# A two-layer model kernel on one Trainium2 core: expert chunks two deep, and gate factors of the last stage made ahead by GpSimd

## The reference, cut to what matters

```python
scores = sigmoid(x @ gate_weight.T)              # 8 experts of 64
topk_w, topk_idx = top_k(scores, 2)
topk_w = topk_w / topk_w.sum(-1) * 2.5           # combine: 0 off the top 2
hmid = silu(x @ w_gate[e]) * (x @ w_up[e])       # and one shared expert pair
out = sum_e combine[:, e] * (hmid[e] @ w_down[e]) + shared
```

```python
mu, var = mean(y), mean((y - mu) ** 2)
yn = (y - mu) * rsqrt(var + 1e-5) * ln_g + ln_b
y = (yn + D_param * u) * silu(z)
x = x + y @ W_out.T
```

```python
h = gelu(sum_e C1[:, e] * (x @ W1[e].T))         # 12 experts
y = sum_e C2[:, e] * (h @ W2[e].T) + C3 @ b2     # 12 experts
```

## Time and profile before

| | |
|---|---|
| median of 3 runs | 1942.43 us (1942.41 to 1942.91) |
| profiled execution, its own time | 1945.75 us |
| its span, first to last instruction | 1943.7 us |
| mean granted PE clock | 0.928 |
| PE busy | 1597.0 us (82%) |
| DVE busy | 1405.3 us (72%) |
| ACT busy | 1012.8 us (52%) |
| POOL busy | 542.6 us (28%) |

### The profile page before, as it was taken

How to read it: one execution, slowest core, us unless ns; L and a number is a source line. 1 busy time by engine, 2 the same in 40 slices (tenths; PEclk the granted TensorE clock), 3 DMA queues, 4 the chain that set the end, 5 groups by cost and what they waited for, 6 DMA issues and landing times. The chain is left out here.

```text
span 1943.7 us, 37126 instructions
## 1 busy us (share of the span) xinstructions
PE 1597.0 (82%) x11024; PEld 1037.9 (53%) x11024; DVE 1405.3 (72%) x3794; ACT 1012.8 (52%) x2725; POOL 542.6 (28%) x556
## 2 busy tenths in 40 slices
PE   6999999999998997889894881776777746787899
PEld 3666666666664554555562771565556533333444
DVE  4777777777776666666675445999999976778776
ACT  2666666666664332232331227999999921221221
POOL 1111111111111010000000111988888856223100
PEclk9999999999999998999896995889888866889999
DMA  4101110111005500000563001000000000000000
GB/s 131 34 22 32 32 32 22 32 32 32 22 22 173 174 0 1 1 0 0 150 202 109 0 0 61 1 1 1 1 1 0 0 0 1 1 6 6 11 6 17
DMA packets 69345, 66.53 MB, mean 34 GB/s; under 512 B 5695, under 2 KB 66834, under 8 KB 69266
## 3 DMA queue, kind: packets, MB, share of 16 engines
q1 hardware_dynamic: 66598, 64.00, 11.1%
q10 hardware_dynamic: 2668, 1.62, 0.3%
HBM read 61.41 MB, written 4.19 MB: 34 GB/s over the span
## 5 line engine op out<-in xcount | busy, mean ns | idle before, releaser
L1968 PE MATMUL ss_y_ps<-ss_h,ss_diag 128*128 128x256 f32 x1024 | 265.3, 423 | 132.9 <-ACT sc_dt L1886 92.7
L1968 PEld LDWEIGHTS ss_y_ps<-ss_h,ss_diag 128*128 128x128 f32 x1024 | 216.5, 215 | 181.4 <-issue 94.6
L595 ACT ACTIVATE x_probs<-x_probs,x_neg_max 128x257 f32<-128x257 f32 x512 | 253.5, 498 | 64.0 <-DVE x_neg_max L696 64.0
L696 DVE CUSTOM_DVE_ANT_0 x_probs<-x_s_ps,x_mask_b 128x257 f32<-128x257 f32 x512 | 187.3, 423 | 134.9 <-PE x_s_ps L403 134.9
L1870 ACT ACTIVATE ss_decay<-sc_dt,sc_a 128x256 f32 (+1 forms) x496 | 206.7, 470 | 1.8 <-DVE ss_h L1933 1.8
L1924 DVE SCALAR_TENSOR_TENSOR ss_decay<-ss_decay,ss_h 128x1024 f32<-128x1024 f32 x124 | 152.3, 1229 | 28.5 <-ACT ss_decay L1870 28.2
L1880 ACT ACTIVATE ss_come<-ss_dtu,sc_xd 128x256 f32<-128x256 f32 x384 | 162.9, 505 | 6.6 <-POOL ss_dtu L1826 6.6
L413 PE MATMUL x_pT_ps<-all_ident,x_probs 128*128 128x128 f32 x1024 | 163.3, 283 | 0.6 <-DVE x_pT L703 0.6
L1840 POOL TENSOR_TENSOR ss_diag<-all_ident,sc_xd 128x512 f32<-128x512 f32 x128 | 159.8, 1249 | 11.4 <-PE ss_y_ps L1968 1.4
L703 DVE COPY x_pT<-x_pT_ps 128x512 f32<-128x512 f32 x256 | 161.3, 668 | 0.5 <-PE x_pT_ps L413 0.5
L1933 DVE CUSTOM_DVE_ANT_0 ss_h<-ss_come,ss_decay 128x1024 f32<-128x1024 f32 x124 | 150.0, 1210 | 0.0
(11 more groups left out here) (371 smaller groups left out, 3134.8 us busy)
## 6 DMA issues: line engine op xcount, KB each, us to landing
x_ctx_t<-ctxT SPq DMA_DIRECT2D x48, 514.0 KB, 3.8
kept_ctx_t<-ctxT SPq DMA_DIRECT2D x16, 514.0 KB, 7.9
kept_ctx_n<-ctx SPq DMA_DIRECT2D x16, 512.0 KB, 8.2
x_ctx_n<-ctx SPq DMA_DIRECT2D x16, 512.0 KB, 4.2
all_x<-x SPq DMA_DIRECT2D x4, 512.0 KB, 7.5
x_mid<-all_x SPq DMA_DIRECT2D x32, 64.0 KB, 4.0
all_x<-x_mid SPq DMA_DIRECT2D x4, 512.0 KB, 7.8
out<-all_x SPq DMA_DIRECT2D x8, 256.0 KB, 2.0
```

Of the source, the lines that this page charges most:

```text
L595: ins = nc.scalar.activation(probs[p][:, n, :], probs[p][:, n, :], ACT.Exp, scale=-1.0, bias=neg_max[p][:, n:n + 1], accum_out=sums[p][:, ...
L696: vec.tensor_tensor_reduce(probs[p][:, n, :], s_ps[:, c, 0:S2], mask_b[:, :], -1.0, -MASKED, ALU.add, ALU.min, neg_max[p][:, n:n + 1]).the ...
L1968: ins = nc.tensor.matmul(y_ps[p][:, 0:DI], diag[q][:, m, :], h[q][:, m, :], start=(q == 0 and m == 0), stop=(q == NQ - 1 and m == NH - 1))
```

## The change

1. **Experts of layer 0.** The loops are written out. `up` is split: `gate_up` (g with a signal of its own for silu, u) and `weigh` (w, which alone waits for the routing weights). `project` runs two chunks behind instead of one, with three buffers for hid. The first two g and u are issued ahead of the first turn of routing weights. The copies of turned x and of turned routing weights move from DVE to ACT. The moments of the finished group go to chunk 4 of the next.
2. **Scan inputs.** The loads of ln_g, ln_b, D_param, w_o, w_a, w_z and b2 move here, behind x on SP. POOL makes for the first 12 tiles (AHEAD = 3 groups) gz = gate * ln_g and q = (u * D_param + ln_b) * gate: four instructions of 128x256 a tile beside its copy.
3. **Tail.** v becomes (y - mean) * gz (`centred`), then * rstd + q (`finish`), eight DVE instructions of 128x256 a group, at steps 17 to 20 of group n for group n+3. POOL makes gz and q of groups 3 to 7 (`gates`), four instructions of 128x1024 each; those of group n+4 start after step 21 of group n (those of group 3 after the first scale of group 0). The norm of x and the copy of the ranks move from DVE to ACT, turn, address and rank to steps 1, 3, 5 (before 3, 5, 8), and the routing two to three steps earlier; the coefficient chain one step later. The prologue projects groups 0 and 1 before it ranks. The three large loads (two halves of w and spread, 768 KB each) are issued at the start of the tail instead of the scan states; PE waits for them before it turns the first weights.

```diff
             pe.wait_ge(g.experts_in, 16 * N_LOADS)
             turn_x(0)
-            logits(0, 0)
+            logits(0)
+            gate_up(0)
+            gate_up(1)
             turn_weights(0)
...
+            def gate_up(i):
+                n, h, b = i // HC, i % HC, i % 2
+                if h == 0:
+                    pe.wait_ge(xT_sb, n + 1)
+                wait(pe, gate_sb, i - 1)
+                mm(g_ps[b][:, :], w_g[:, h, :], xnT[n % 2][:, :], start=True, stop=True).then_inc(gate_psum, 1)
+                wait(pe, hid_sb, i - 1)
+                ins = mm(u_ps[b][:, :], w_u[:, h, :], xnT[n % 2][:, :], start=True, stop=True)
...
+                for h in range(HC):
+                    if n * HC + h >= 2:
+                        gate_up(n * HC + h)
+                        weigh(n * HC + h)
+                    if n * HC + h >= LAG0:
+                        project(n * HC + h - LAG0)
...
+            def gates(t, p):
+                keep(t, p)
+                pool.wait_ge(uz_sb, t + 1)
+                nc.gpsimd.tensor_tensor(tw.gz[:, t, :], uz[:, t, DI:2 * DI], tw.ln_g[:, :], ALU.mult).then_inc(tw.gz_sb, 1)
+                nc.gpsimd.tensor_tensor(tw.q[:, t, :], uz[:, t, 0:DI], tw.d_p[:, :], ALU.mult).then_inc(tw.q_sb, 1)
+                pool.wait_ge(tw.q_sb, 3 * t + 1)
+                nc.gpsimd.tensor_tensor(tw.q[:, t, :], tw.q[:, t, :], tw.ln_b[:, :], ALU.add).then_inc(tw.q_sb, 1)
+                pool.wait_ge(tw.q_sb, 3 * t + 2)
+                nc.gpsimd.tensor_tensor(tw.q[:, t, :], tw.q[:, t, :], uz[:, t, DI:2 * DI], ALU.mult).then_inc(tw.q_sb, 1)
...
+            sp.dma_start(spread[:, :, :].rearrange("r e n -> r (e n)"), g.dram["c_spread1"]).then_inc(tw.loaded, 16)
+            sp.dma_start(w[:, 0:ME, :], g.dram["L1_W1_T"]).then_inc(tw.loaded, 16)
+            sp.dma_start(w[:, ME:MC, :], g.dram["L1_W2_T"]).then_inc(tw.loaded, 16)
             for n in range(NG):
...
+            def gates(m):
+                pool.wait_ge(scaled_sb, 1 if m == AHEAD else (m - AHEAD - 1) * MC + MC - 2)
+                pool.wait_ge(mid_step, (m - AHEAD) * GT + GT)
+                nc.gpsimd.tensor_tensor(gated(m), uz[:, tiles(m), DI:2 * DI], every(ln_g), ALU.mult).then_inc(gz_sb, 1)
...
-            pool.wait_ge(tw.loaded, 16 * TAIL_LOADS)
-            skips(0)
-            skips(1)
-            finish(1)
-            for m in range(2, NG):
-                skips(m)
-                finish(m)
+            for m in range(AHEAD, NG):
+                gates(m)
...
+            pe.wait_ge(tw.loaded, 16 * TAIL_LOADS)
             turn_weights(0)
             for n in range(NG):
                 group(n)
...
+            def norm(m):
+                act.wait_ge(coef, chain_base(m) + chain_steps(m))
+                wait(act, xT_psum, m)
+                for k in range(GT):
+                    nc.scalar.activation(xn[:, k, :], g.x[:, m * GT + k, :], ACT.Identity, bias=sh[:, m + 2, k:k + 1],
+                                         scale=rs[:, m + 2, k:k + 1]).then_inc(xn_ready, 1)
...
+                for k in ks:
+                    vec.scalar_tensor_tensor(v[:, k, :], y[:, m * GT + k, :], sh[:, m, GT + k:GT + k + 1],
+                                             gated(m)[:, k, :], ALU.subtract, ALU.mult).then_inc(mid_step, 1)
...
+                for k in ks:
+                    vec.scalar_tensor_tensor(v[:, k, :], v[:, k, :], rs[:, m, GT + k:GT + k + 1], skip(m)[:, k, :],
+                                             ALU.mult, ALU.add).then_inc(v_sb, 1)
```

More of the change, by code:

```diff
@@ L1344, in _ @@
             norm(0)
-            copy_xT(0, 0)
             routing_top(0)
             routing_weights(0)
-            copy_weights(0, 0)
-            group(0, 0, False, True)
-            with dve.Fori(0, NG // 2 - 1) as i:
-                group(i * 2 + 1, 1, True, True)
-                group(i * 2 + 2, 0, True, True)
-            group(NG - 1, 1, True, False)
+            for n in range(NG):
+                for h in range(HC):
+                    hidden(n * HC + h)
+                    if n + 1 < NG:
+                        if h == 0:
+                            norm(n + 1)
+                        if h == 2:
+                            routing_top(n + 1)
+                        if h == 3:
+                            routing_weights(n + 1)
+                    if n and h == LAG0 - 1:
+                        add_out(n - 1)
+                    if n and h == 4:
+                        moments(n - 1)
             add_out(NG - 1)
+            moments(NG - 1)
             dve.wait_ge(stats_sb, T)
@@ L2239, in _ @@
             project(0)
+            turn_v(1, 0)
+            turn_v(1, 1)
+            project(1)
             turn_x(0)
@@ L2498, in moments_next, with gated_next @@
                     chain_e(c)
[L2500 to L2504 removed]
+            def gated_next(m, j):
+                if j == 17:
+                    centred(m, (0, 1))
+                if j == 18:
+                    centred(m, (2, 3))
+                if j == 19:
+                    finish(m, (0, 1))
+                if j == 20:
+                    finish(m, (2, 3))
+            y_stats(0, range(GT))
+            chain_a(-2)
+            chain_b(-2)
+            chain_c(-2)
+            centred(0, range(GT))
+            chain_d(-2)
+            finish(0, (0, 1))
+            finish(0, (2, 3))
+            y_stats(1, range(GT))
+            chain_a(-1)
+            chain_b(-1)
+            chain_c(-1)
+            centred(1, range(GT))
+            chain_d(-1)
+            finish(1, (0, 1))
+            finish(1, (2, 3))
             y_stats(2, range(GT))
@@ L2521, in _ @@
             chain_c(1)
+            centred(2, range(GT))
+            finish(2, (0, 1))
+            finish(2, (2, 3))
+            dve.wait_ge(pads, 3)
+            for k in range(2):
+                lists(0, k)
+            chain_d(1)
+            chain_e(1)
+            for k in range(2):
+                marks(0, k)
+            exponents(0)
             totals(0)
```

381 lines of the change are left out of this document (172 added, 209 removed).

## The result

The changed kernel takes 1870.34 us (median of four, 1869.71 to 1872.8) where the kernel before takes 1942.67 (four runs beside it); the ratio is 0.9629, 95% interval 0.9613 to 0.9646. The forecast was 1869 in 1852 to 1892. The profiled execution has a span of 1868.5, against 1943.7: 75.2 shorter. (The profiled execution of before was 3 us above its median, so 72 to 75 is the gain.)

What follows compares the result with a forecast made beforehand. The prediction saw PE with waits bounding the first experts and DVE steps slowed by POOL bounding the tail. Terms -24 + 1 - 20.5 - 30 = -73.5 took the median from 1942.43 to 1869 us, range 1852 to 1892.

Steps and rivals of the forecast that it cites:

- First experts, -24: Experts of layer 0: a group's period falls from 19.05 to 16.0 us, so the stage gains 24 us.
- What bounds the kernel now: Opening section: experts are PE work with 2.2 us of waits a group; the tail's DVE steps are slowed by POOL.
- The lag of two gives hidden one more chunk of time: Experts of layer 0: projecting two chunks behind gives hidden 2.82 us more room than before.
- the lag does nothing: Rival, experts of layer 0: u waits for hidden two chunks back, only the start's 4 us remain; 1889 us, chance 0.07.
- Scan inputs, +1: Scan inputs: POOL falls behind 0.25 us a tile, two u buffers cover it; cost taken as 1 us.
- upper end: Scan inputs: DVE's two steps a tile hold POOL up, it falls behind 1.3 us a tile, cost 10 us.
- Prologue, -20.5: Tail from its start to the first gelu: 63.4 instead of 84.0 us, a gain of 20.5.
- Groups, -30: Tail, five gaps from gelu to gelu carrying v work: 35.8 us each, 179.0 together, a gain of 30.
- The 8 us of room: Tail groups: the first small DVE step, the coefficient chain at step 9, stands some 8 us after POOL's gates end.
- PE's own pace (33.9): Rival, tail groups: all five gaps take 33.9 us, gaining 39.4 instead of 30; 1860 us, chance 0.15.
- The collision elsewhere: Rival, tail groups: gates drag past step 9 or meet the routing, gaps stay at 45; 1899 us, chance 0.08.
- The big loads: Slower case, tail: three loads issued at its start eat the whole gain if landing after 110 us; chance 0.02.

## Why the prediction was right, point by point

**First experts, -24 (measured -23.7).** The size was right and the period too (16.0 forecast, 15.83 in most groups, 16.18 in the last), g(2) came at 781.61 (781.9 forecast, though in a stage that began 1.9 earlier), and PE's wait for e_weightT is gone from the row of g. The reason was right in part only. The period was taken between 15.6, PE's own work, and 16.4, the old period less its waits, and the three waits that "What bounds the kernel now" names for a group, for xn, for the parts and for the weights' copy, are the ones that went (0.82, 0.50 and 0.86 in the earlier trace rows). What does not hold is the step "The lag of two gives hidden one more chunk of time": undoing the lag costs 3.7 us, and what PE then waits for in the later groups is the add on x, not `hidden`. In the kernel before, too, a project waited more than 0.15 us for `hidden` only in the first group (0.20) and at the very end (0.52). The prediction took the change as one thing, and so its rival "the lag does nothing" was priced at 1889, as if nothing but the early start were left; the kernel with a lag of one in fact still has a stage of 141.4 + 3.7. Undone one at a time, the weights' wait is worth 1.0 a group and the wait for the parts 0.5. The latter went because silu no longer waits for w:

```profile
L1259 ACT ACTIVATE e_gate<-e_g_ps 128x512 f32<-128x512 f32 x40 | 23.9, 597 | 40.6 <-PE e_g_ps L1192 40.5
```

Idle 40.6 instead of 105.9, and it is g that ends it, not w.

**Scan inputs, +1 (measured -0.3).** POOL starts most tiles 3.71 to 3.73 us apart, over all twelve 3.80, in a period of 3.58; it falls behind 0.22 a tile (0.25 forecast), and the u buffers cover it. Both engines hold each other up, POOL and then DVE:

```profile
1045.88 1.02 POOL L1756 TENSOR_TENSOR sc_q<-sc_q,sc_uz 128x256 f32<-128x256 f32 x1
1046.84 0.61 POOL L1746 COPY sc_uz<-si_u 128x512 f32<-128x512 f32 x1
...
1050.55 0.61 POOL L1746 COPY sc_uz<-si_u 128x512 f32<-128x512 f32 x1
```

```profile
1045.82 0.48 DVE L1785 SCALAR_TENSOR_TENSOR sc_dt<-si_w_dt,sc_xd,si_b_dt 128x256 f32<-128x256 f32 x1
1046.22 0.75 DVE L1776 TENSOR_SCALAR si_xn<-all_x,all_rstd,all_shift 128x128 f32<-128x128 f32 x1
```

POOL's step at 1045.88 takes 1.02 instead of 0.73, because DVE's began 0.06 ahead of it; DVE's next takes 0.75 instead of 0.34 behind POOL's. So here POOL was held up too, the direction that the rows of before did not show, as the Trainium skill has it ("SBUF — State Buffer", "Who interferes with whom": whoever issues first), but it costs POOL 0.3 now and then and not the 1.05 a tile of the upper end.

**Prologue, -20.5 (measured -21.2).** First v turned 5.0 after the start (4.6 forecast), first spread 39.1 (38.7), first gelu 62.8 (63.4; 61.0 in some kernels with the same tail, last section). No small DVE step stands any more:

```profile
1549.17 0.16 DVE L2376 SCALAR_TENSOR_TENSOR tl_lnw<-tl_lnw 128x4 f32<-128x4 f32 x1
1549.25 0.16 DVE L2379 TENSOR_SCALAR tl_lnw<-tl_lnw 128x4 f32<-128x4 f32 x1
1549.32 0.16 DVE L2382 TENSOR_SCALAR tl_sh<-tl_lnw 128x4 f32<-128x4 f32 x1
1549.52 0.16 DVE L2387 TENSOR_TENSOR tl_lnw<-tl_lnw 128x4 f32<-128x4 f32 x1
1549.60 1.67 DVE L2407 SCALAR_TENSOR_TENSOR tl_v<-sc_dt,tl_sh,sc_gz 128x256 f32<-128x256 f32 x4
```

The first of these is the step that took 2.23 in the earlier trace rows.

**Groups, -30 (measured -28.0).** 36.2 a gap instead of 35.8. A term that was too small is the new DVE work: four steps of 128x256 take 1.67, 0.42 each, where a quarter of the 1.23 of a 128x1024 step had been taken, 0.31. Eight of them make 0.9 us of DVE a group more; that this is what makes the gap 0.4 longer was not tried. The 8 us of room between the gates and the chain were there: gates 1659.16 to 1668.69, first coefficient step 1676.83.

**The rivals.** PE's own pace (33.9) was not reached: the changed kernel's gaps hold 33.97 of PE and 2.3 of waits, at the end of DVE's dense stretch and behind gelu. The collision elsewhere did not come, and the kernel with late gates shows by how much it can: 3.7 to 4.4 a gap with the gates in the routing. The big loads were no wait: from 1547 to 1562 us, in 40 slices of 0.375, the DMA engines moved (GB/s)

```profile
GB/s 0 0 0 49 213 66 360 426 442 426 393 426 442 410 410 426 410 442 426 360 164 0 0 0 0 0 0 0 0 0 0 0 0 0 0 0 0 0 0 0
```

and were done at 1554.9, 29 us ahead of the first turn of weights at 1584.17, behind which PE would have stood.

## What to carry to other kernels

Where one engine's instruction can stop another's, place their work by time and not by amount: 9.4 us of GpSimd work cost next to nothing where VectorE ran scales, adds and moments, and 4 us a group where three small steps of VectorE stood beside it. Before a wait is moved ahead, look at what is queued behind it in order: a stall of 6 us on one engine became 10 for the kernel. And when a change has several parts, undo them one by one before naming a cause, and read in each kernel what is waited for: undoing the lag brought back a wait for the add on x and not the wait for `hidden` for which it was made.

## What the runs showed of the hardware that was not expected

The same tail code had one of two prologues, 61 or 63 us to the first gelu (60.9 to 61.2 in five kernels, 62.8 to 63.0 in three), with the gaps behind it the same to 0.1, but for two gaps of one kernel. In both the instructions start alike up to the second projection. Then, in the profile of the changed kernel (the first two rows) PE stays slow, and in the one with a lag of one in the experts (the other two) it gets faster within it:

```profile
1565.58 3.79 PE L2170 MATMUL tl_o_ps<-sc_w_o,tl_vT 128*128 128x128 f32 x16 [3.54 <-ACT tl_vT L2275]
1569.15 1.06 PE L2177 MATMUL tl_m_ps<-all_ident,tl_xn 128*128 128x128 f32 x4
```

```profile
1566.50 3.58 PE L2170 MATMUL tl_o_ps<-sc_w_o,tl_vT 128*128 128x128 f32 x16 [3.08 <-ACT tl_vT L2275]
1569.91 0.60 PE L2177 MATMUL tl_m_ps<-all_ident,tl_xn 128*128 128x128 f32 x4
```

The granted clock of the prologue is 0.59 in the one and 0.65 in the other, that is the lower of its two levels (1.2 of 2.4 GHz) for most of it. The two differ in when it rises, again first the one, then the other:

```profile
1564.40:1591.50 27.10, 13.79 (x47) 9.70 (x48) 15.74 (x81) 8.11 (x17) 3.57 (x2) 0.50 0.00 1
```

```profile
1569.90:1576.40 6.50, 2.76 (x16) 1.53 (x14) 6.07 (x27) 2.86 (x5) 0.00 (x0) 1.00 0.00 0
1576.70:1590.00 13.30, 4.37 (x16) 2.77 (x17) 7.83 (x49) 3.53 (x8) 2.28 (x1) 0.50 0.00 1
```

Nothing in the tail differs between the two kernels. What decides when the clock rises was not found; it is worth 1.9 us, as much as some of the edits measured here.
